# Biases of q, k and the first feed-forward layer: added by ScalarE during eviction instead of by products on TensorE

## What is computed

```python
# first cross-attention, one head: scores of normalised x against the context, softmax, added to x
# gate: a softmax over 4 experts of the mean of the normalised x; the 2 best are chosen
# 16 sequences x 2 chosen experts = 32 "units", each an encoder layer with the expert's weights:
def _encoder_layer(x, iw, ib, ow, ob, l1w, l1b, l2w, l2b, n1w, n1b, n2w, n2b):
    qkv = x @ iw.T + ib                          # 16 heads of 16
    scores = einsum('bhqd,bhkd->bhqk', q, k) / scale
    o = softmax(scores) @ v ...
    x = _layernorm(x + o @ ow.T + ob, n1w, n1b)
    ff = relu(x @ l1w.T + l1b) @ l2w.T + l2b     # 256 -> 1024 -> 256
    return _layernorm(x + ff, n2w, n2b)
# causal cross-attention of x with the context (16 more units, without a feed-forward layer)
# a shared gated feed-forward layer for all tokens, and one of 8 experts for 512 chosen tokens
```

## Time and profile before

| | before |
|---|---|
| median of 3 runs | 840.95 us (839.58 to 840.96) |
| the profiled execution: its own time | 838.61 us |
| its span | 836.8 us |
| mean granted clock of TensorE | 0.932 |
| busy: TensorE, weight loads | 730.0 us (87%), 580.5 us (69%) |
| busy: VectorE, ScalarE, GpSimd | 650.5 us (78%), 337.1 us (40%), 378.6 us (45%) |
| instructions of ScalarE | 710 |

### The profile page before, as it was taken

One profiled execution on the slowest core, in us unless ns is written; L12 is line 12 of the kernel. 1 busy time (PEld: TensorE's weight loads), 2 busy tenths in 40 slices (PEclk: granted clock), 3 DMA queues, 4 the chain that ended last, 5 costly groups with the idle time before them and its releaser, 6 DMA issues.

```text
span 836.8 us, 29143 instructions
## 1 busy us (share of the span) xinstructions
PE 730.0 (87%) x10976; PEld 580.5 (69%) x10976; DVE 650.5 (78%) x1858; ACT 337.1 (40%) x710; POOL 378.6 (45%) x647
## 2 busy tenths in 40 slices
PE   6978569999999999999999999998889888734895
PEld 5767547888888888888888888875556656412673
DVE  4686555878878797787878788879999999845865
ACT  4665324343443434344343444344445445411200
POOL 1788613344453544445353454542354445245132
PEclk9996579999999999999999999999999999955797
DMA  7677400000000000000000000002322222122000
GB/s 270 221 223 243 158 1 3 3 3 4 2 3 2 3 3 4 3 2 4 3 3 4 3 4 9 9 22 64 99 78 70 77 90 72 39 81 79 6 1 6
DMA packets 24651, 41.22 MB, mean 49 GB/s; under 512 B 3725, under 2 KB 16663, under 8 KB 24265
## 3 DMA queue, kind: packets, MB, share of 16 engines
q1 hardware_dynamic: 23096, 37.39, 13.7%
q0 software_dynamic: 704, 1.71, 0.7%
q10 hardware_dynamic: 722, 0.28, 0.1%
HBM read 30.85 MB, written 8.91 MB: 48 GB/s over the span
## 4 chain that ended last, share of the span: by engine, by line
PE 66%; DVE 16%; POOL 7%; issue 7%; ACT 3%; DMA 1%; POOLq 0%; ACTq 0%; DVEq 0%; SPq 0%
PE ps L475 7%; PE ps L469 7%; PE ps L477 6%; PE ps L476 6%; PE ps L670 6%; PE ps L652 5%; DVE mx L1389 5%; PE ps L602 4%; PE ps L708 3%; POOL w_lo L1812 3%; PE ps L710 3%; PE ps L709 3%; PE ps L604 3%; PE ps L603 3%; PE ps L594 2%
## 5 line engine op out<-in xcount | busy, mean ns | idle before, releaser
L1026 ACT ACTIVATE pT<-ps 128x1024 f32<-128x1024 f32 x96 | 93.1, 1021 | 126.1 <-PE ps L652 126.1
L1785 POOL TENSOR_TENSOR rs<-mv,cst 128x1 f32<-128x1 f32 x132 | 31.0, 235 | 179.7 <-DVE mv L1160 142.0
L1389 DVE TENSOR_REDUCE mx<-ps 128x16 f32<-128x2048 f32 x48 | 109.5, 2281 | 1.0 <-PE ps L625 1.0
L1873 POOL TENSOR_TENSOR y<-y,vec 128x256 f32<-128x256 f32 x32 | 23.2, 724 | 171.0 <-DVE y L1163 171.0
L708 PE MATMUL ps<-xh,w_hi 128*128 128x128 bf16 x512 | 99.4, 219 | 0.1
L709 PE MATMUL ps<-xl,w_hi 128*128 128x128 bf16 x512 | 99.3, 219 | 0.0
L710 PE MATMUL ps<-xh,w_lo 128*128 128x128 bf16 x512 | 99.2, 219 | 0.0
L1787 POOL TENSOR_TENSOR rs<-rs,cst 128x1 f32<-128x1 f32 x132 | 73.0, 553 | 10.3
L475 PE MATMUL ps<-w_hi,hh 128*128 x256 | 69.8, 273 | 0.0
L477 PE MATMUL ps<-w_lo,hh 128*128 x256 | 69.8, 273 | 0.0
L476 PE MATMUL ps<-w_hi,hl 128*128 x256 | 69.8, 273 | 0.0
(11 more groups left out here) (364 smaller groups left out, 2510.9 us busy)
## 6 DMA issues: line engine op xcount, KB each, us to landing
stage<-in_w SPq DMA_DIRECT2D x32, 384.0 KB, 3.7
vec<-in_vec SPq DMA_DIRECT2D x4, 896.0 KB, 5.9
vec<-in_tw SPq DMA_DIRECT2D x12, 256.0 KB, 2.7
ctxc<-in_ctx SPq DMA_DIRECT2D x19, 128.0 KB, 2.3
comb<-x SPq DMA_DIRECT2D x16, 128.0 KB, 1.7
comb<-t SPq DMA_DIRECT2D x16, 128.0 KB, 1.8
shared<-x1b SPq DMA_DIRECT2D x16, 128.0 KB, 1.7
out<-x SPq DMA_DIRECT2D x16, 128.0 KB, 1.8
```

The costliest lines, as they stand in the source:

```text
L1026: A(pT[:, 8 * a:8 * a + 8, :].rearrange("p h q -> p (h q)"), ps[:, 2 * a:2 * a + 2, :].rearrange("p g k -> p (g k)"), ACT.Exp, scale=SCALE ...
L1389: nc.vector.tensor_reduce(mx[:, :], att.rearrange("p g s k -> p (g s) k"), AX.X, ALU.max, negate=True).then_inc(m_max, 1)
```

## The change

The biases leave TensorE. They come in as columns, one value per partition and 128 outputs (`bcol`, 12 columns per expert and 12 for the causal attention), and ScalarE adds them while it evicts PSUM to SBUF in fp32, 128 columns at a time, since each block of 128 outputs has its own column: `qk_full` writes `qf` and `kf`, `relu` writes `hfs`. The high parts are then cast from these fp32 copies and the low parts subtracted from them. The column is picked by the unit's expert, so ScalarE now loads the words with the chosen experts as the other engines did. In the causal blocks the high parts are made straight from PSUM with the bias (`qk_hi_causal`; for k, whose two halves are masked, the bias is masked beforehand in `kmb`), and the fp32 copy is made later. Waits change too: PSUM's bank 4 is free once `qk_full` has run (`qk_sb`), and banks 6 and 7 once the relu is in SBUF (`hr_b`, `hr_a`). Some small tensors of the last stage move into `ones`, which is not used there.

ScalarE in an expert block, before: from the eviction of the attention's output (`ctxb` is `oT`) on to the next exponentials.

The diff, cut to its core:

```diff
-K_SEL, K_CS, K_CT, K_ROW = 0, 512, 640, 768
-NROW = E + 1
-K_ALL = K_ROW + NROW
-B_QK = DFF
-B_ALL = DFF + 2 * D
+K_SEL, K_CS, K_CT, K_ALL = 0, 512, 640, 768
+B_QK, B_EXP = FC, FC + 2 * KC
...
-        b1hl = sb("b1hl", [128, B_ALL], bf16)
+        bcol = sb("bcol", [128, B_ALL])
+        kmb = sb("kmb", [128, 2 * KC])
...
+        hf = sb("hf", [128, FC // 2, 128])
+        hfs = (hf[:, :, :], h[:, 512:1024].rearrange("p (c k) -> p c k", k=128))
+        qf = sb("qf", [128, KC, 128])
+        kf = sb("kf", [128, KC, 128])
...
-            def projection_qk(k, base, e):
+            def projection_qk(k, base):
 
                 pe.wait_ge(yT_ready, k + 1)
                 for j in range(4):
                     dst = ps[:, 4, 128 * j:128 * j + 128]
-                    mm(dst, b1hl[:, B_QK + 128 * j:B_QK + 128 * j + 128], row_of(e), start=True, stop=False)
                     for c in range(KC):
                         src = KC + c if base is None and j >= 2 else c
                         off = W_QKV + c * 3 * D + 128 * j
...
-                        mm(dst, w1, ycT_hi[:, src, :], start=False, stop=False)
+                        mm(dst, w1, ycT_hi[:, src, :], start=(c == 0), stop=False)
                         mm(dst, w1, ycT_lo[:, src, :], start=False, stop=False)
                         last = mm(dst, w2, ycT_hi[:, src, :], start=False, stop=(c == KC - 1))
...
                 for j in range(4):
-                    b0 = 512 * half + 128 * j
                     dst = ps[:, 7 - half, 128 * j:128 * j + 128]
-                    mm(dst, b1hl[:, b0:b0 + 128], row_of(e), start=True, stop=False)
                     for c in range(KC):
-                        mm(dst, w(w_hi, c, j), xh[:, c, :], start=False, stop=False)
+                        mm(dst, w(w_hi, c, j), xh[:, c, :], start=(c == 0), stop=False)
                         mm(dst, w(w_hi, c, j), xl[:, c, :], start=False, stop=False)
                         last = mm(dst, w(w_lo, c, j), xh[:, c, :], start=False, stop=(c == KC - 1))
...
                 if half == 1:
                     pe.wait_ge(hl_b, u + 1)
+                    pe.wait_ge(hr_a, u + 1)
+                else:
                     pe.wait_ge(hl_a, u + 1)
...
                 if not isinstance(m, int) or m > 2:
-                    pe.wait_ge(hl_b, m - 2)
-                projection_v(None if causal_m else ex(1)[0])
+                    pe.wait_ge(hr_b, m - 2)
+                projection_v(None if causal_m else ex(1))
...
                 if kp is not None:
-                    pe.wait_ge(qk_split, m + 1)
+                    pe.wait_ge(qk_sb, m + 1)
                     prep(kp, isinstance(kp, int) and kp >= B)
...
+                    out_proj(n, None if causal_n else ex(0))
                 if next_k is not None:
-                    pe.wait_ge(qk_split, m + 1)
-                    base, e = (None, E) if causal(n + 2) else ex(2)
-                    projection_qk(next_k, base, e)
+                    pe.wait_ge(qk_sb, m + 1)
+                    projection_qk(next_k, None if causal(n + 2) else ex(2))
...
             def ex_of(u):
-                e = digit(words_pe[u // WORD], u % WORD)
-                return e * W_EXP, e
-            projection_qk(0, *ex_of(0))
+                return digit(words_pe[u // WORD], u % WORD) * W_EXP
+            projection_qk(0, ex_of(0))
...
+            def bias_of(u, j):
+                e0 = E * B_EXP if causal(u) else digit(words_act[u // WORD], u % WORD) * B_EXP
+                return bcol[:, ds(e0 + j, 1)]
+
+            def qk_full(u):
+
+                act.wait_ge(qk_psum, u + 1)
+                if u > 0:
+                    act.wait_ge(qk_split, u)
+                for j in range(2 * KC):
+                    dst = (qf if j < KC else kf)[:, j % KC, :]
+                    last = A(dst, ps[:, 4, 128 * j:128 * j + 128], ACT.Identity, bias=bias_of(u, B_QK + j))
+                last.then_inc(qk_sb, 1)
+
             def qk_hi(u):
+                act.wait_ge(qk_sb, u + 1)
+                copy(qh[:, :, :], qf[:, :, :])
+                for s in range(2):
+                    last = A(khm[:, :, s, :], kf[:, :, :], ACT.Copy, scale=mask_eo[s])
+                last.then_inc(qkT_hi, 1)
+
+            def qk_hi_causal(u):
+
                 act.wait_ge(qk_psum, u + 1)
-                copy(qh[:, :, :], ps[:, 4, 0:D].rearrange("p (c k) -> p c k", k=128))
-                kk = ps[:, 4, D:2 * D].rearrange("p (c k) -> p c k", k=128)
+                for c in range(KC):
+                    A(qh[:, c, :], ps[:, 4, 128 * c:128 * c + 128], ACT.Identity, bias=bias_of(u, B_QK + c))
                 for s in range(2):
-                    last = A(khm[:, :, s, :], kk, ACT.Copy, scale=mask_eo[s])
+                    for c in range(KC):
+                        last = A(khm[:, c, s, :], ps[:, 4, D + 128 * c:D + 128 * c + 128], ACT.Identity,
+                                 bias=kmb[:, 2 * s + c:2 * s + c + 1], scale=mask_eo[s])
                 last.then_inc(qkT_hi, 1)
...
             def relu(u, half):
                 act.wait_ge(h_b if half else h_a, u + 1)
-                A(hh[:, 4 * half:4 * half + 4, :], ps[:, 7 - half, :].rearrange("p (c k) -> p c k", k=128),
-                  ACT.Relu).then_inc(hh_b if half else hh_a, 1)
+                if u > 0:
+                    act.wait_ge(hl_b if half else hl_a, u)
+                for j in range(FC // 2):
+                    last = A(hfs[half][:, j, :], ps[:, 7 - half, 128 * j:128 * j + 128], ACT.Relu,
+                             bias=bias_of(u, FC // 2 * half + j))
+                last.then_inc(hr_b if half else hr_a, 1)
+                act.wait_ge(hr_b if half else hr_a, u + 1)
+                copy(hh[:, 4 * half:4 * half + 4, :], hfs[half]).then_inc(hh_b if half else hh_a, 1)
...
+                if attends(n):
+                    oo(n)
                 if encodes(f):
                     relu(f, 1)
-                if attends(n):
-                    oo(n)
                 shift(m)
                 if encodes(f):
                     relu(f, 0)
+                if n < UNITS:
+                    qk_full(n + 2)
...
                     exps(n)
                 if served(b + 1):
-                    qk_hi(m)
+                    qk_hi_causal(m)
                 if served(b):
                     o_evict(n)
+                if served(b + 1):
+                    qk_full(m)
...
+            act.wait_ge(b1_in, 16)
+            act.wait_ge(g_words, 1)
+            words_act = [word_of(act, 0)]
+            qk_full(0)
             for n in range(-1, UNITS + 1):
+                if n % WORD == WORD - 4 and n // WORD + 1 < UNITS // WORD:
+                    words_act.append(word_of(act, n // WORD + 1))
                 block(n, prep_of(n + 2))
+            act.wait_ge(vones_ready, 6)
...
                 weights_quarter(i)
-                if i == 3:
-                    dve.wait_ge(b1_hi, 1)
-                    for c0, width, rows_f in b1f:
-                        tt(b1hl[32:32 + NROW, c0:c0 + width], rows_f, b1hl[0:NROW, c0:c0 + width],
-                           ALU.subtract).then_inc(b1_ready, 1)
...
                     for slot in range(2):
                         nc.vector.memset(v2[slot][:, :, HD:HD + 1], 1.0).then_inc(vones_ready, 1)
+                    dve.wait_ge(b1_in, 16)
+                    for s in range(2):
+                        ts(kmb[:, 2 * s:2 * s + 2], bcol[:, E * B_EXP + B_QK + KC:B_ALL], mask_eo[s], None,
...
             def qk_low(u):
                 dve.wait_ge(qkT_hi, u + 1)
-                tt(ql[:, :, :], ps[:, 4, 0:D].rearrange("p (c k) -> p c k", k=128), qh[:, :, :], ALU.subtract)
-                kk = ps[:, 4, D:2 * D].rearrange("p (c k) -> p c k", k=128)
+                dve.wait_ge(qk_sb, u + 1)
+                tt(ql[:, :, :], qf[:, :, :], qh[:, :, :], ALU.subtract)
                 for s in range(2):
-                    last = stt(klm[:, :, s, :], kk, mask_eo[s], khm[:, :, s, :], ALU.mult, ALU.subtract)
+                    last = stt(klm[:, :, s, :], kf[:, :, :], mask_eo[s], khm[:, :, s, :], ALU.mult, ALU.subtract)
                 last.then_inc(qk_split, 1)
...
             def h_low(u, half):
                 dve.wait_ge(hh_b if half else hh_a, u + 1)
-                stt(hl[:, 4 * half:4 * half + 4, :], ps[:, 7 - half, :].rearrange("p (c k) -> p c k", k=128), 0.0,
-                    hh[:, 4 * half:4 * half + 4, :], ALU.max, ALU.subtract).then_inc(hl_b if half else hl_a, 1)
+                tt(hl[:, 4 * half:4 * half + 4, :], hfs[half], hh[:, 4 * half:4 * half + 4, :],
+                   ALU.subtract).then_inc(hl_b if half else hl_a, 1)
...
-              cat([np.zeros(DFF, np.float32), at["bq"], at["bk"]])[None, :]])
+              cat([np.zeros(DFF, np.float32), at["bq"], at["bk"]])[None, :]]).reshape(B_ALL, 128).T
     e12 = cat([cat([f1["ew1"][e], f1["ew2"][e]]).T for e in range(EM)], axis=1)
```

53 lines of the change are left out of this document (18 added, 35 removed).

## The result

| | before | after |
|---|---|---|
| median of 4 runs | 840.27 us (837.17 to 840.96) | 893.62 us (892.90 to 894.69) |
| the profiled execution: own time, span | 838.61, 836.8 us | 893.82, 891.9 us |
| mean granted clock of TensorE | 0.932 | 0.907 |
| busy: TensorE, VectorE | 730.0, 650.5 us | 734.4, 687.5 us |
| busy: ScalarE, GpSimd | 337.1, 378.6 us | 468.0, 406.1 us |

The changed kernel takes 1.0655 times as long, with a 95% interval of 1.0627 to 1.0682: 53 us more. The forecast was 875 us with a range of 852 to 893. The direction was right, the time lies 0.6 us beyond the range, and the surplus is half as large again as forecast.

The account below looks back on a forecast made before the run. The prediction had full engines waiting for each other at fixed points: TensorE for VectorE and GpSimd (expert stage), VectorE behind ScalarE (causal stage). -1.5 + 6 + 26 + 2.5 + 1 = +34 us on 838.6 gave 872.6, as median 875; range 852 to 893.

Parts of the forecast that it names:

- the mechanism of the causal stage: Causal blocks: VectorE's ql waits for ScalarE's late fp32 copy, 1.85 us in each of 14 blocks, +26 us.
- the maxima move by the same: Causal blocks: the maxima shift by VectorE's whole 1.75 to 1.95 us stall, so each block grows by it.
- TensorE's clock falls: Rival: longer causal pauses drop 2.4 to 1.2 GHz in a third of blocks, some 4 us each, +19, 894; 5%.
- the term of a pair: Expert stage, two blocks: 0.75 lateness - 0.1 slack - 2 x 0.15 products = 0.35 us, +6 us over 16 pairs.
- the lateness of x1: Expert stage, every other block: GpSimd's x1 0.75 us late, from second h_low 0.5 late plus 0.25 of collisions.
- an expert block gains 0.15 us: Expert stage: removed bias products save 0.15 us per block, bounds 0.03 and 0.6.
- The low-clock blocks: First blocks after 104 us, partly at half clock: TensorE is later than VectorE, so 1.5 us gained, bounds 0 and 3.
- the two fixed points: Expert stage: TensorE waits for VectorE's ool before L475 and, every other block, GpSimd's x1; slack about 0.1 to 0.17 us.
- Start: Before the first cast of qh: a load of the expert word and four copies add +2.5 us, bounds 1.2 and 4.
- TensorE as the bound: Rival: TensorE sets the time throughout, so all 24.9 us of products are saved, 816 us; 6%.
- a gaining expert stage: Rival: causal stall comes, but relu's lateness stays covered and each of 32 expert blocks gains 0.5 us, 853; 16%.
- Collisions: Rival: VectorE and GpSimd block each other at each h_low, +12 over 16 pairs, klm +4, 891 us; 11%.

Follow-up runs that it names:

- w_lo later: The changed kernel, with GpSimd's w_lo subtraction in the causal blocks waiting until the maxima and their split are done; 873.67 us, ratio 1.0407.
- VectorE's order: The changed kernel, with VectorE in the causal blocks doing gate product, shared sum and o's norm before q's and k's low parts; 884.9 us, ratio 1.0531.
- fillers: The changed kernel plus 28 unused identity products on TensorE in each causal block from the second on; 885.99 us, ratio 1.0554.
- both edits: The changed kernel with VectorE's causal order changed and GpSimd's w_lo held until the maxima are split; 865.78 us, ratio 1.0321.
- without products: The kernel before with the 448 bias products left out and nothing in their place; 836.75 us, ratio 0.9981.
- q and k from PSUM everywhere: The changed kernel without the fp32 copy of q and k in causal and expert blocks, k's bias dropped, relu still four instructions; 852.19 us, ratio 1.0144.

## Why the prediction was right and wrong

**Right: the mechanism of the causal stage and its size.** "VectorE stands 1.75 to 1.95 us", maxima "about 14.0 us apart". With w_lo out of the way and the clock steady the period is 14.01 (12.13 before): 197.8 - 173.8 = 24 us, forecast 26. The second and third causal block of the changed kernel, which have no w_lo yet, show it too: 13.66 and 13.91. A little luck is in the agreement: VectorE stands 2.2 us, not 1.85, and wins 0.25 us back between ql and the maxima (2.87 us before, 2.62 with w_lo later), which the forecast had kept fixed.

**Failed: the sum of the causal stage, 26 for 44.5 us.** Its two missing terms are each measured by one experiment: 9.9 us for the gate product (L1569) held by w_lo in 11 of the 14 blocks (0.9 each), 10.5 us for seven falls of the clock. 24.0 + 9.9 + 10.5 = 44.4. The failed step is "the maxima move by the same": I shifted VectorE's queue by the stall and let everything behind it keep its length. The period grew by 2.8 us in the blocks at full clock and by about 4.3 in the seven with a fall. The rows for a check were there. L1547 with w_lo 0.16 us behind it stands in the trace of before, and so do its two durations of 1.00 us with w_lo 0.3 us ahead, in the last two causal blocks. The earlier trace rows showed what two SBUF operands cost beside GpSimd; its median of 493 ns hides that 15 of the 32 took 790 ns or more. The prediction applied the lock only to h_low and klm, and asked of no other pair whose order would turn. It turned because GpSimd's sum waits for L1588, which the stall delays, and w_lo follows that sum directly: both engines now start from the same event, and GpSimd wins by 0.11 us. In the two blocks of before GpSimd's sum had waited in the same way (0.63 us).

**Failed: the chance of the clock.** "TensorE's clock falls" had 5% and +19 us ("in a third of the blocks, some 4 us each"). It fell seven times in 14 blocks, at 1.5 each. The price per block was too high and the chance far too low. I had let the one pause before the shift grow by the whole stall, and there are two pauses. TensorE's waits in the causal stage of the changed kernel:

```profile
PE ps L624 <- DVE mtile L1419: 27.1, 13, 2.3
PE ps L473 <- DVE xl L1550: 24.8, 14, 2.2
```

Before, only the first existed (19.6 us in 13 blocks), the second was 0.4 us in all. The second, 1.8 us a block, is the stall itself, seen from TensorE. The first is 1.40 us with w_lo later and 2.31 in the changed kernel, so the collision of the gate product lengthens it by 0.9 us; that is how holding w_lo back can bear on the clock. Between 600 and 740 us the longest of these pauses was 2.3 us after and with VectorE's order (both fell) and 1.8, 1.8 and 1.4 us with w_lo later, with fillers and with both edits (none fell), while the pauses' sum was nearly the same with the order (31.7 us, fell) and with w_lo later (32.0, didn't). It isn't the longest pause alone: without products the first fall came 0.9 us after a pause of 1.76 us, shorter than those that w_lo later and the fillers went through without a fall, and the kernel before went through one of 2.1 us. What exactly tips it stays open; that it hangs on the idle time around the stall is shown by the fillers. By the Trainium skill, TensorE: Matmul & The Clock Gate, in its part on a second HAM failure mode (psum-queue depth-cycling), a kernel's clock went back and forth because TensorE idled briefly and often between its groups of products. The trace is in keeping with it: no pause of the causal stage ahead of a fall was longer than 2.3 us.

**Expert stage: +5.5 forecast, +9.3 measured.** TensorE waits where it was forecast to, 16 times. Two sizes in the term of a pair were off. The first is the lateness of x1, forecast at 0.75 us in every other block: the block shown above has 0.87. Its parts differ more than their sum. ScalarE was to make the second h_low 0.5 us late and VectorE's collisions were to add 0.25; where the first half isn't held, the second starts only 0.25 to 0.30 us late, and the collision adds more than the 0.25 granted, 0.5 us in the duration of the first half. The second size is the credit: "an expert block gains 0.15 us" from the missing products, 0.3 per pair. The run without products gives 26.56 us for a pair against 26.61, so the gain is 0.05: the block without a transposition does gain 0.18, and the other gives 0.13 back. 0.87 - 0.1 - 0.05 = 0.72 would have been the term, and a pair measures 27.33 - 26.61 = 0.72. (The low-clock blocks: M0 to M4 takes 52.7 us for 53.8, a gain of 1.1 where 1.5 was forecast.) The argument for nought stood in the text (TensorE follows VectorE at L475 and GpSimd at x1); I took a compromise where the two fixed points left almost none.

**Start: +2.5 forecast, +2.2 in this pair of profiles.** But M0 lies at 104.7, 105.0 and 107.0 us in the three profiles of kernels that start like before, and at 108.5 to 110.0 in the nine that load the word on ScalarE, so the term is more like +3.5. The kernel with q and k from PSUM everywhere makes no copy there and still starts its maxima at 109.1, so the forecast's 1.15 us for four copies is borne out by nothing. The loads of words, those at the start and the +1 for the later ones, weren't measured apart, nor was the 0.08 us for a semaphore of ScalarE on itself shown by any row; the cast starts 0.02 us behind the relu's four pieces.

**Rivals.** TensorE as the bound (816) and a gaining expert stage (853) are refuted by the run without products. Collisions (891) was right in kind and in part in place. In the expert stage h_low's first half is held in most blocks (median 1150 ns), against my argument from the median of the earlier trace rows, but only one half of a tail is held, not both, and in the blocks without a transposition it costs nothing. klm isn't held in the causal blocks (0.87 us). The costlier collision was the gate product's, in the causal stage. The result is the forecast's mechanism with a collision and the clock on top. I had treated collisions and clock them as alternatives to it, though the stall makes both likelier, and so the upper end of the range (893) left out the case in which they come together.

**The signs.** VectorE's wait ahead of ql (2.2 us), the relu's spacing and TensorE's wait for x1 came as listed. The causal period of 14.0 came only once w_lo and the clock were out of the way, and the expert period is 13.67 on average, just above the 13.4 to 13.6. One sign of being wrong came true as it was written: a clock below 1.00 between 150 and 700 us.

## What to carry to other kernels

When a change stalls one engine, don't only shift its queue: list each instruction behind the stall whose duration depends on who comes first (two SBUF operands on VectorE, any tensor instruction on GpSimd), write down the lead in the trace of before, and treat a lead smaller than the stall as open (here 0.16 us against a stall of 2.2). Read a line's durations one by one: a median hides that every other one is held. Where TensorE's new pauses come on top of old ones, give its clock a real chance to fall, and put such consequences on top of the stall in the range rather than beside it. Work removed from an engine that follows others at fixed points earns little (2.4 us for 448 products that would fill 24.9 by my estimate from the earlier trace rows), whatever its busy share.

## What the runs showed of the hardware

- Idle products can be worth their time. With 28 of them per block the clock stayed at 1.00 in a kernel that otherwise fell seven times, and the stage took 10.5 us less. Each of the seven falls between M33 and M47 lasted 3.4 us and cost 1.5. The reverse, that removing products lets the clock fall, rests on one trace: without the 448 bias products it fell three times in the last causal blocks (0.87 over 683 to 725 us), but two other kernels without them fell once and not at all in that stage.
- The lock between VectorE and GpSimd turns on tenths of a microsecond: the same pair took 0.36 us with VectorE 0.16 ahead and 1.19 with GpSimd 0.11 ahead. It follows the order of the queues, so moving one instruction handed the lock to another (klm, 0.87 to 1.76 us for two). It can alternate within one line: the line of the earlier trace rows took 474 to 505 ns in 17 of its 32 instances and 790 to 996 in the others.
- ScalarE with a per-partition bias from PSUM: 128 columns 375 to 382 ns, with 0.25 us from start to start (four in 1.15 us), and 0.34 with a per-partition scale as well (four in 1.52), so cutting 512 columns into four costs 0.55 us over one instruction of 0.60.
